# Linear attention on one core: two biases leave TensorE for VectorE, and the order inside a tile changes

## What is computed

```python
q = heads(x @ Wq.T + bq); k = heads(x @ Wk.T + bk); v = heads(x @ Wv.T + bv)
g = sigmoid(heads(x @ Wg.T + bg))
q = elu(rope(q)) + 1;  k = elu(rope(k)) + 1          # 16 heads of 32
for each chunk of 64 tokens:                          # S, Z carried along
    S += k.T @ v;  Z += sum(k)
    out = g * (q @ S) / (q @ Z + 1e-6)
x = layernorm(x + (out @ Wo.T + bo))
```

## Time and profile before

| | us |
|---|---|
| median of 3 runs | 1068.72 (1068.3 to 1070.1) |
| the profiled execution, its own time | 1067.34 |
| its span | 1065.5 |
| PE busy | 990.8 (93%) |
| DVE busy | 707.8 (66%) |
| start of q_transposed, tile 0 | 31.29 |
| first product of the mixture stage | 365.50 |

### The profile page before, as it was taken

How to read it: one execution, slowest core, us unless ns; L and a number is a source line. 1 busy time by engine, 2 the same in 40 slices (tenths; PEclk the granted TensorE clock), 3 DMA queues, 4 the chain that set the end, 5 groups by cost and what they waited for, 6 DMA issues and landing times.

```text
span 1065.5 us, 14065 instructions
## 1 busy us (share of the span) xinstructions
PE 990.8 (93%) x5432; PEld 777.2 (73%) x5432; DVE 707.8 (66%) x1166; ACT 403.5 (38%) x623; POOL 293.2 (28%) x245
## 2 busy tenths in 40 slices
PE   5899898999998589999999999999999999999996
PEld 4677676777776457777777778778777777788885
DVE  7546966876776678486659768647958765555433
ACT  5233533433433333444442434342444444222231
POOL 4268784543353102001321101322200132000031
PEclk9899998999999779999999999999999999999999
DMA  8136663210110172344451434381333445153421
GB/s 285 65 147 227 250 227 132 89 30 21 50 51 31 49 272 90 133 154 174 167 207 40 168 116 166 114 308 53 124 138 140 152 150 181 40 196 125 173 70 58
DMA packets 47857, 142.92 MB, mean 134 GB/s; under 512 B 3624, under 2 KB 14632, under 8 KB 42160
## 3 DMA queue, kind: packets, MB, share of 16 engines
q1 hardware_dynamic: 28720, 118.71, 30.8%
q10 hardware_dynamic: 19072, 23.32, 6.8%
HBM read 114.63 MB, written 27.39 MB: 133 GB/s over the span
## 4 chain that ended last, share of the span: by engine, by line
PE 45%; DVE 14%; ACT 2%; issue 2%; DMA 2%; POOL 1%; DVEq 0%; ACTq 0%
PE f_h L104 8%; PE f_h L105 8%; PE f_h L106 8%; PE f_h L2210 4%; PE f_y L104 2%; PE f_y L106 2%; PE f_y L105 2%; DMA f_down_raw<-in_down_stream 2%; DVE f_work L1949 2%; DVE f_q_mem L1969 2%; PE f_y L2407 1%; DVE f_row_max L2019 1%; DVE f_work L1941 1%; PE f_z_sum L104 1%; PE f_z_sum L105 1%
## 5 line engine op out<-in xcount | busy, mean ns | idle before, releaser
L104 PE MATMUL f_h<-f_xT_hi,f_up 128*128 128x512 f32 x352 | 140.5, 399 | 0.0
L105 PE MATMUL f_h<-f_xT_hi,f_up 128*128 128x512 f32 x352 | 138.6, 394 | 0.0
L106 PE MATMUL f_h<-f_xT_lo,f_up 128*128 128x512 f32 x352 | 137.8, 392 | 0.0
L104 PE MATMUL ring<-w_hi,xT_hi 128*128 128x512 f32 x256 | 110.8, 433 | 19.5 <-DVE w_lo L722 10.8
L1521 POOL TENSOR_TENSOR f_down_lo<-f_down_raw,f_down_hi 128x512 fp32r<-128x512 f32 x44 | 59.8, 1358 | 236.5 <-ACT f_down_hi L1573 236.5
L1735 ACT ACTIVATE f_work<-f_h 128x512 f32<-128x512 f32 x88 | 52.5, 596 | 179.4 <-PE f_h L2210 119.7
L1941 DVE TENSOR_TENSOR f_work<-f_work,f_weightT 128x512 f32<-128x512 f32 x88 | 64.7, 735 | 70.6 <-ACT f_work L1735 70.3
L1532 POOL TENSOR_TENSOR weights<-weights,f_rows 128x512 f32<-128x512 f32 (+1 forms) x24 | 32.2, 1374 | 284.2 <-ACT f_rows L1658 184.7
L1949 DVE TENSOR_TENSOR f_work<-f_h,f_work 128x512 f32<-128x512 f32 x88 | 60.8, 691 | 67.8 <-PE f_h L106 62.6
L106 PE MATMUL ring<-w_lo,xT_hi 128*128 128x512 f32 x256 | 103.5, 404 | 0.0
L105 PE MATMUL ring<-w_hi,xT_lo 128*128 128x512 f32 x256 | 103.1, 403 | 0.0
(11 more groups left out here) (315 smaller groups left out, 2161.7 us busy)
## 6 DMA issues: line engine op xcount, KB each, us to landing
f_up<-up_scratch SPq DMA_DIRECT2D x44, 1408.0 KB, 6.0
f_down_raw<-in_down_stream ACTq DMA_DIRECT2D x44, 256.0 KB, 3.7
x_tok<-x_scratch SPq DMA_DIRECT2D x7, 1024.0 KB, 9.4
scaled_w<-in_up_stream SPq DMA_DIRECT2D x6, 704.0 KB, 5.2
up_scratch<-q_mem SPq DMA_DIRECT2D x6, 704.0 KB, 4.9
up_scratch<-scaled_w SPq DMA_DIRECT2D x6, 704.0 KB, 3.1
x_tok<-in_x SPq DMA_DIRECT2D x4, 1024.0 KB, 5.7
out<-x_tok SPq DMA_DIRECT2D x8, 512.0 KB, 3.1
```

The source lines that it names most:

```text
L104: pe.matmul(out, lhs_hi, rhs_hi, start=start, stop=False)
L105: pe.matmul(out, lhs_lo, rhs_hi, start=False, stop=False)
L106: return pe.matmul(out, lhs_hi, rhs_lo, start=False, stop=stop)
```

## The change

The biases of v and of the gate are no longer products on TensorE. Two transfers bring them, spread over the 128 partitions, into a new tile `vg_bc`, and VectorE adds them as it takes the sums from their banks: `v_out` moves from ScalarE to VectorE, and a new `gate_sum` writes the biased gate into SBUF, where ScalarE's tanh reads it. The order inside a tile changes on three engines, with two forms: one for tiles below `LIGHT = 7`, one for the others.

```diff
+LIGHT = 7
@@ sync engine, after the second weight's chunks @@
                     sp.dma_start(bo_bc[:, :], bo).then_inc(bo_loaded, 16)
+                    for i in range(2):
+                        sp.dma_start(vg_bc[:, i, :], bias_rows[4 + 2 * i:5 + 2 * i, :].to_broadcast([P, D]))\
+                            .then_inc(vg_loaded, 16)
@@ ScalarE @@
-            def v_out(g):
...
             def gate_out(g):
                 k, _, done = own(g, PG)
-                act.wait_ge(filled[k], done)
-                if 2 * g:
-                    act.wait_ge(gated, 2 * g)
-                act.activation(gate[:, :], ring[k][:, :], ACT.Tanh, scale=0.5).then_inc(drained[k], 1)
...
+                act.wait_ge(drained[k], done)
+                act.activation(gate[:, :], gate[:, :], ACT.Tanh, scale=0.5).then_inc(gate_ready, 1)
+
+            def exponential(g, i):
+                act.wait_ge(neg_ready, 2 * g + i + 1)
...
                 if more:
                     qk_out(g + 1, PK)
+                if has_next(g, 2):
+                    x_hi(g + 2)
...
-                if more:
-                    v_out(g + 1)
+                if g < LIGHT:
+                    exponential(g + 1, 0)
...
                 attT_hi(g)
-                if more:
-                    exponential(g + 1)
+                if g < LIGHT:
+                    exponential(g + 1, 1)
+                elif more:
+                    exponential(g + 1, 0)
                 if g == 13:
                     quantised(1, 0)
+                if more and g >= LIGHT:
+                    exponential(g + 1, 1)
                 if more:
                     gate_out(g + 1)
                 if has_next(g, 3):
                     load_xT(g + 3)
-                if has_next(g, 2):
-                    x_hi(g + 2)
@@ VectorE @@
-                k, _, done = own(g, PG)
-                dve.wait_ge(drained[k], done)
+                dve.wait_ge(gate_ready, g + 1)
...
+            def v_out(g):
+                k, _, done = own(g, PV)
+                dve.wait_ge(filled[k], done)
+                if g:
+                    dve.wait_ge(s_updated, 2 * g)
...
+                dve.tensor_tensor(v_ext[:, g % 2, :, 0:DK], ring[k][:, :].rearrange("p (h e) -> p h e", e=DK),
+                                  vg_bc[:, 0, :].rearrange("p (h e) -> p h e", e=DK), ALU.add)\
+                    .then_inc(drained[k], 1)
+
+            def gate_sum(g):
+                k, _, done = own(g, PG)
+                dve.wait_ge(filled[k], done)
+                if g:
+                    dve.wait_ge(gated, 2 * g)
+                dve.tensor_tensor(gate[:, :], ring[k][:, :], vg_bc[:, 1, :], ALU.add).then_inc(drained[k], 1)
...
             for g in range(TILES):
+                mask_state(g, 1)
                 if g == 5:
                     channel_top(0, 0)
...
-                mask_state(g, 1)
                 if g == 7:
                     channel_scale(0)
...
                 attend(g)
                 if has_next(g):
                     rotated_sum(g + 1, 0)
+                if g < LIGHT:
+                    rotated_sum(g + 1, 1)
...
+                if has_next(g):
+                    v_out(g + 1)
                 attT_lo(g)
...
                 if has_next(g):
-                    rotated_sum(g + 1, 1)
+                    if g >= LIGHT:
+                        rotated_sum(g + 1, 1)
                     features(g + 1, 0)
                     features(g + 1, 1)
...
+                if has_next(g):
+                    gate_sum(g + 1)
@@ TensorE: project(g, item, channels) runs the given row blocks c; last is its last product @@
+                    last = matmul_split(pe, ring[k][:, :], xT_hi[:, g % 2, c, :], xT_lo[:, g % 2, c, :],
+                                        w_hi[:, i, c, :], w_lo[:, i, c, :], c == 0, i > 1 and c == KT - 1)
...
+                if item in (PV, PG):
+                    last.then_inc(filled[k], 1)
+                    return
...
                 if more:
-                    project(g + 1, PQ)
+                    project(g + 1, PQ, (0, 1))
                 update_state(g, 1)
                 if more:
+                    project(g + 1, PQ, (2, 3))
+                if g < LIGHT:
+                    numerators(g)
+                if more:
                     project(g + 1, PK)
-                numerators(g)
+                if g >= LIGHT:
+                    numerators(g)
```

More of the change, by code:

```diff
@@ L181, in attention_and_experts @@
         bo_bc = sb("bo_bc", [P, D])
+        vg_bc = sb("vg_bc", [P, 2, D])
         x_tok, stats = shared.x_tok, shared.stats
@@ L239, in attention_and_experts @@
         bo_loaded = sem("bo_loaded")
+        vg_loaded = sem("vg_loaded")
+        gate_ready = sem("gate_ready")
         w_loaded = [[sem(f"w_loaded{i}_{c}") for c in range(KT)] for i in range(5)]
@@ L539, in qk_out @@
                     .then_inc(drained[k], 1)
-            def v_out(g):
-                k, _, done = own(g, PV)
-                act.wait_ge(filled[k], done)
-                if 2 * g:
[L545 to L549, removed]
             def gate_out(g):
                 k, _, done = own(g, PG)
-                act.wait_ge(filled[k], done)
-                if 2 * g:
-                    act.wait_ge(gated, 2 * g)
-                act.activation(gate[:, :], ring[k][:, :], ACT.Tanh, scale=0.5).then_inc(drained[k], 1)
[L558 to L562, removed]
+                act.wait_ge(drained[k], done)
+                act.activation(gate[:, :], gate[:, :], ACT.Tanh, scale=0.5).then_inc(gate_ready, 1)
+            def exponential(g, i):
+                act.wait_ge(neg_ready, 2 * g + i + 1)
+                half = bass.ts(i, D)
+                act.activation(rot_b[:, half], rot_b[:, half], ACT.Exp).then_inc(exp_ready, 1)
             def qT_out(g):
@@ L651, in _ @@
             load_xT(2)
-            v_out(0)
             weight_hi(4)
-            exponential(0)
+            exponential(0, 0)
+            exponential(0, 1)
             gate_out(0)
@@ L806, in attend @@
                     .then_inc(att_ready, 1)
+            def v_out(g):
[3 more added lines that the diff above has]
+                    dve.wait_ge(s_updated, 2 * g)
+                else:
+                    dve.wait_ge(vg_loaded, 32)
+                if g < 2:
+                    dve.wait_ge(v_ones_ready, 2)
+                dve.tensor_tensor(v_ext[:, g % 2, :, 0:DK], ring[k][:, :].rearrange("p (h e) -> p h e", e=DK),
[7 more added lines that the diff above has]
+                dve.tensor_tensor(gate[:, :], ring[k][:, :], vg_bc[:, 1, :], ALU.add).then_inc(drained[k], 1)
             def attT_lo(g):
@@ L953, in _ @@
                 features(0, i)
+            v_out(0)
+            gate_sum(0)
             mask_state(0, 0)
             for g in range(TILES):
+                mask_state(g, 1)
                 if g == 5:
@@ L1031, in _, with project @@
         def _(pe):
-            def project(g, item):
+            def project(g, item, channels=range(KT)):
                 k, free, _ = own(g, item)
                 i = (PQ, PK, PV, PG).index(item)
-                if item == PQ:
-                    pe.wait_ge(xlo_ready, g + 1)
-                if free:
-                    pe.wait_ge(drained[k], free)
-                for c in range(KT):
+                if 0 in channels:
+                    if item == PQ:
+                        pe.wait_ge(xlo_ready, g + 1)
+                    if free:
+                        pe.wait_ge(drained[k], free)
+                for c in channels:
                     if g == 0:
                         pe.wait_ge(w_lo_ready, KT * i + c + 1)
-                    matmul_split(pe, ring[k][:, :], xT_hi[:, g % 2, c, :], xT_lo[:, g % 2, c, :],
-                                 w_hi[:, i, c, :], w_lo[:, i, c, :], c == 0, False)
+                    last = matmul_split(pe, ring[k][:, :], xT_hi[:, g % 2, c, :], xT_lo[:, g % 2, c, :],
+                                        w_hi[:, i, c, :], w_lo[:, i, c, :], c == 0, i > 1 and c == KT - 1)
+                if KT - 1 not in channels:
+                    return
+                if item in (PV, PG):
+                    last.then_inc(filled[k], 1)
+                    return
                 if g == 0:
```

## The result

The changed kernel takes 1083.09 us (median of 4 runs, 1081.48 to 1087.8) against 1069.41 for the kernel before beside it (4 runs). The ratio is 1.0133, with a 95% interval of 1.0112 to 1.0153: 14 us slower, where a gain of 4 was forecast, and outside the range of 1055 to 1071. The profiled execution took 1081.48, its span is 1079.7.

What follows compares the result with a forecast made beforehand. TensorE's order was taken to set the attention stage's time, plus its waits and clock falls. Terms by tile summed to -4.3 us, 1063.0 for the profiled execution, median forecast 1064.4; range 1055 to 1071, likeliest case 1060.5 to 1066.5.

Steps and rivals of the forecast that it cites:

- the replay of a tile below 7: Timeline from a tile's opening: `attT_lo` ends at 15.9 to 16.2, `output` 1.2 us late, tile 18.8 us.
- the sum by tile: Gains and losses of tiles 0 to 15 added up to -4.3 us against the profiled execution.
- some 0.3 us later again: Tiles below 7: by the port rule alone, VectorE's pair could wait for GpSimd, making `output` some 0.3 us later.
- The price of a bias: Every tile: two VectorE instructions added, about 0.6 each in a row, for two TensorE products removed, 0.46 a tile.
- Tile 0: Products save 0.46, late `output` adds 1.2, the first update's wait for `v_out` 0.15: +0.9 us.
- The clock: Tile 7: if the clock stays up, another 2.2 go; -2.0 us taken, bounds -0.8 and -3.2.
- Tiles 5 and 6: A chain over a transfer, not TensorE, sets the end of tile 6: 43.0 us against 43.71, -0.7.
- Tiles 7 to 14: Tile 7 -2.0, tile 8 +1.4, tile 9 -1.2, tile 11 +1.5, tile 12 -0.6, tile 13 -2.8 us.
- no wait for `xT_lo` anywhere: All tiles: x is rounded two projections earlier, so TensorE's waits for its remainder vanish.
- the two transfers: Ahead of the third weight's chunks: 512 KB costed at nothing, up to 2 us if the cover is gone.
- C: Rival, slower: VectorE becomes the bound, features late in tiles 7 to 14, 1.3 each: about 1073 us; chance 0.19.
- D: Rival: x's remainder still late, 0.9 in tiles 2 to 5: 1067 us; chance 0.20 jointly with nothing measurable.

Runs made afterwards that it cites:

- late_wait: The changed kernel with the wait for GpSimd's rotated half moved behind the cosine product in rotated_sum: 1078.2 us, ratio 1.0077.
- order_only: The changed kernel's new order, with both biases left as products on TensorE and both sums taken by ScalarE: 1071.3 us, ratio 0.9998 to the kernel before.
- gate_on_dve: The changed kernel with v's bias back on TensorE and v's sums taken by ScalarE; the gate's bias stays on VectorE: 1077.3 us, ratio 1.0089.
- order_late: order_only with the wait for the rotation moved behind the cosine product: 1065.7 us, ratio 0.9957 to the kernel before.
- after_fill: The changed kernel with eight useless products on TensorE ahead of the wait before `output` in tiles 0 to 6: 1079.4 us, ratio 1.0095.
- v_behind: The changed kernel with `v_out` behind `attT_lo` on VectorE in place of ahead of it: 1085.0 us, ratio 1.0137.
- light0: The changed kernel with LIGHT = 0, so the k half goes back behind `attT_lo` in every tile: 1084.0 us, ratio 1.0128.
- xhi_only: The kernel before with one edit, the rounding of x moved on ScalarE to behind the copy of k: 1072.5 us, ratio 1.0028.

## Why the prediction was wrong

The steps that failed are the replay of a tile below 7, which left the cosine product off the path to `attT_lo`, and the sum by tile, which priced the two biases at nearly nothing outside a few named waits and allowed for no new fall of the clock.

- **The replay of a tile below 7.** Forecast 18.8, measured 20.62 to 20.64 in tiles 1 to 3. The step is "From there GpSimd goes straight on to its next task, and the pair costs ... 1.78 + 1.40: 14.7 to 15.0". The pair took 1.66 + 1.10 and is no error; in front of it stood the cosine product, 1.77, which the replay had nowhere on the path. The code says so: the wait comes first. `attT_lo` ended at 17.7, not 15.9 to 16.2. late_wait, which moves only this wait, gives 5 to 6 us back. The "some 0.3 us later again" that the prediction adds for a rule has no working behind it, and the pair, 2.76 for the forecast 3.18, does not show it.
- **The price of a bias.** Two adds at 0.6 for two products at 0.23 each is already a loss on a tile where VectorE leads to the end. The sum had `v_out` in most tiles, but `gate_sum` only where a wait for it could be seen in advance. Tile 2 shows v's undisturbed: the wait for `att_lo` is 1.08 longer than in order_only (2.78 and 1.70), two products are saved, and the tile is 0.59 longer (20.62 and 20.03). The gate's costs nothing there (20.04 in gate_on_dve), but 2.0 and 2.4 in tiles 4 and 8 (23.25 and 24.16, for 21.27 and 21.81), where a mask is late; tile 8 has a fall besides. Over the stage, the changed kernel has 11.7 more idle than order_only.
- **Tile 0.** Forecast 21.2, measured 24.31, the largest miss of one tile. Both kernels open it at the lower level, behind a wait of 4.56 and 4.86. Before, the clock was up 5 us later, now 10 us later, and the products in between cost about 2.4, by what is left of the miss. The wait for `att_lo`, 1.87 for the forecast 1.2, is the rest. The late rise is not the biases': order_late, without them, has it too (0.78, 23.49), and order_only has not (0.89, 21.56). Why it comes in some traces stays open.
- **The clock.** The sum allowed for one fall to vanish in tile 7 and for none to come. Tile 7 did better than its bound of -3.2 (-3.9, full clock). But tiles 4, 5, 6 and 8 each had a fall of some 3.5 us to the lower level, behind waits of 2.10, 2.71, 2.11 and 1.79. At 0.43 between products in place of 0.23, such a fall costs about 1.7. And the fall of tile 12, behind the wait of 3.2 for the gate's sum, was longer than before (0.86 for 0.92). The prediction's reading that only tiles 0, 7 and 9 had falls overlooked that one. In tile 4 the terms are: the wait for `att_lo` 1.3 over the forecast (2.52), the mask's 0.9 under it (2.10 for 3.0), and the fall 1.7. Together they make 2.1 of the 2.3 by which the tile missed.
- **Tiles 5 and 6.** Forecast 43.0 for both, held by the chain over the transfer; measured 44.8, with no large wait at the opening of tile 7. TensorE, with its two falls, was later than that chain. In after_fill, without the falls, they took 43.3 and tile 7 waited 1.24 for the gate's sum, which is the chain as forecast.
- **Tiles 7 to 14.** Tile 8's wait for the mask (1.79 for 2) and its 0.56 for `att_lo` were right; it took 24.39 for 22.3, and 22.79 in after_fill, which had no fall there. Tile 9 took 22.84 for 20.5; a bank was overlooked there: the gate's projection takes the bank of v, which VectorE now drains behind `attend`, 2.33 of wait. In tile 11 the forecast was +1.5, measured +2.4, with the wait for the gate's sum as described (3.2). Tile 13 gained 1.5, not 2.8: the wait for `q_mem` fell from 2.51 to 0.2, but the mask is 1.07 late.
- **Right**: no wait for `xT_lo` anywhere; the places of the waits named for tiles 4, 8 and 11; the two transfers cost nothing that can be seen (tile 0 opens 1.25 earlier, and between 30.0 and 31.9 in all traces).
- **The rivals.** C, VectorE as the bound, was the right mechanism, but placed only from tile 7 on, and its point of decision was put at the features. Its time, 1073, was 10 short. The runs put it below tile 7 too, and at `att_lo` as much as at the features. Late_wait, v_behind and light0 together show it: each move of an instruction on VectorE changes which wait appears. D did not occur.

In tiles 1 to 3 the clock is full, so their loss is idle time alone, and late_wait and order_only put it down to the step in the replay and to v's bias. How much of the stage's remaining loss is idle time and how much the clock can't be split exactly, since a fall also delays what comes next. The 2.5 us lost behind the stage are not explained; there the 14 profiled executions took 700.0 to 703.7 us, xhi_only 701.6 without any bias on VectorE, so they may be no effect of the change.

## What to carry to other kernels

Read an instruction's waits in the code before placing it in another's shadow: one wait too early in a helper cost as much here as the whole forecast gain. Moving an add from an engine that is 93% busy to one that is 66% busy pays only if the second has slack in that stretch; ask that per tile, backwards from the instruction that the first engine waits for. And if TensorE is at its limit, a new wait of 2 us can cost more than 2 us: give the fall of the clock a term in the range, since it comes behind some waits and not behind others.

## What the hardware showed that was not expected

- A wait can be paid twice, but one can't tell by its length. Behind the waits of 1.79, 2.10, 2.11 and 2.71 above the clock fell to 1.2 GHz for some 3.5 us, and in the kernel before already behind 1.49 and 1.54 (the openings of tiles 12 and 9). Behind 1.70 in order_only it did not, nor behind three of 2.78 in tiles 1 to 3 of the changed kernel, with full clock all along. The wait of tile 8 was 1.79 with a fall and 1.80 without (after_fill). Behind the two waits that work of no use filled down to 0.9 or less, the fall did not come; this is one trace, and tile 8 shows that a fall can also stay away by itself.
- The cosine product on VectorE took 0.91, 1.35 and 1.77 us for one shape in tile 2 of three kernels, by what GpSimd did beside it (0.67 at the least in the kernel before), and GpSimd's product with the sines (L439, now L448) 1.29 and 1.75. The Trainium skill, SBUF — State Buffer, "Who interferes with whom", says that an instruction of VectorE with two inputs in SBUF contends with GpSimd's reads; the traces agree: both engines' instructions are longer where they overlap, and 1.77 against 0.91 is the size seen here.
